# Two attention layers in one kernel: a unit's eight transposes in one place instead of two

## The reference, cut to what matters

```python
# layer 0, per sample
q, k, v = Wq @ y + bq, Wk @ y + bk, Wv @ x + bv          # y = ctx
a = softmax(q_h @ k_h.T / sqrt(E))                       # 8 heads of 32 channels
o = Wo @ (a @ v_h) + bo + x
x1 = (o - mean(o)) * rsqrt(var(o) + eps) * gn_w + gn_b   # over the whole sample
# layer 1, per sample, in chunks of 64 positions
q, k, v = (W_in @ y + b_in).split(3)
p = softmax(q_h.T @ k_h / sqrt(32) + (mask ? 0 : -1e9))  # 64 x 64 per head and chunk
z = (W_out @ (p @ v_h) + b_out) * mask + x1
out = (z - mean(z)) * rsqrt(var(z) + eps)                # over the 2048 positions of a channel
```

## Time and profile before

| | |
|---|---|
| median of 3 runs | 1703.49 us (1701.91 to 1703.87) |
| own time of the profiled execution | 1699.56 us |
| its span from first to last instruction | 1697.7 us |
| mean granted clock of TensorE | 0.988 |
| busy: TensorE, VectorE, ScalarE, GpSimd | 1572.2, 1345.1, 990.8, 471.7 us |

### The profile page before, as it was taken

One profiled execution on the slowest core, in us unless ns is written; L12 is line 12 of the kernel. 1 busy time (PEld: TensorE's weight loads), 2 busy tenths in 40 slices (PEclk: granted clock), 3 DMA queues, 4 the chain that ended last, 5 costly groups with the idle time before them and its releaser, 6 DMA issues.

```text
span 1697.7 us, 56577 instructions
## 1 busy us (share of the span) xinstructions
PE 1572.2 (93%) x23816; PEld 1313.9 (77%) x23816; DVE 1345.1 (79%) x2006; ACT 990.8 (58%) x1779; POOL 471.7 (28%) x293
## 2 busy tenths in 40 slices
PE   3999999999999999999999999999999999999982
PEld 3887787878778787787878778788787878878772
DVE  2777978878787897978878787797978878787884
ACT  3566475565656566475565656566465565656552
POOL 0113224142331313224141331314224142331313
PEclk9999999999999999999999999999999999999996
DMA  5222231323314232231323314232231323314021
GB/s 208 89 74 84 88 105 66 126 82 113 101 45 133 69 125 83 88 105 66 126 82 113 101 45 129 73 122 86 88 109 62 126 82 112 102 46 135 11 76 50
DMA packets 96167, 158.26 MB, mean 93 GB/s; under 512 B 5329, under 2 KB 38225, under 8 KB 95697
## 3 DMA queue, kind: packets, MB, share of 16 engines
q1 hardware_dynamic: 95952, 154.83, 27.8%
HBM read 121.25 MB, written 33.55 MB: 91 GB/s over the span
## 4 chain that ended last, share of the span: by engine, by line
PE 69%; DVE 16%; ACT 8%; issue 5%; DMA 1%; POOL 0%; SPq 0%; ACTq 0%; DVEq 0%; POOLq 0%
PE pj_ps L280 30%; PE l_ps L280 11%; PE l_ps L384 6%; PE s_ps L304 5%; PE w_ps L333 4%; PE w_ps L315 4%; DVE y_lo L675 3%; DVE o_sb L814 2%; ACT y_hi L523 2%; DVE prob L700 2%; PE l_ps L400 2%; ACT o_sb L572 2%; PE s_ps L293 2%; PE l_ps L420 2%; DVE att_lo L717 1%
## 5 line engine op out<-in xcount | busy, mean ns | idle before, releaser
L894 POOL TENSOR_TENSOR prob<-prob,row_inv 128x1024 f32<-128x1024 f32 x128 | 260.1, 2032 | 1001.7 <-DVE row_inv L710 1001.7
L582 ACT CAST att_hi<-w_ps 128x256 fp32r<-128x256 f32 x256 | 82.6, 375 | 292.6 <-PE w_ps L333 288.1
L280 PE MATMUL pj_ps<-y_hi,w_hi 128*128 128x512 f32 x512 | 208.6, 407 | 3.7 <-DVE y_lo L675 3.7
L280 PE MATMUL pj_ps<-y_hi,w_lo 128*128 128x512 f32 x512 | 202.4, 395 | 0.0
L280 PE MATMUL pj_ps<-y_lo,w_hi 128*128 128x512 f32 x512 | 202.4, 395 | 0.0
L693 DVE TENSOR_REDUCE row_max<-s_ps 128x16 f32<-128x1024 f32 x128 | 156.0, 1219 | 56.4 <-PE s_ps L304 54.7
L705 DVE TENSOR_REDUCE row_sum<-prob 128x16 f32<-128x1024 f32 x128 | 154.9, 1210 | 42.6 <-ACT prob L564 42.6
L559 ACT COPY prob_t<-w_ps 128x512 f32<-128x512 f32 x256 | 149.8, 585 | 37.7 <-PE w_ps L315 34.9
L911 POOL TENSOR_TENSOR o_sb<-o_sb,u_sb 128x1024 f32<-128x1024 f32 x64 | 165.6, 2610 | 1.6 <-ACT o_sb L572 1.6
L315 PE MATMUL w_ps<-cst,prob 128*128 128x128 f32 x1024 | 146.9, 274 | 19.2 <-DVE att_lo L717 19.0
L700 DVE TENSOR_TENSOR prob<-s_ps,row_max 128x1024 f32<-128x1024 f32 x128 | 155.3, 1213 | 2.0 <-issue 1.9
(11 more groups left out here) (105 smaller groups left out, 3578.8 us busy)
## 6 DMA issues: line engine op xcount, KB each, us to landing
y_raw<-in_ctx SPq DMA_DIRECT2D x64, 512.0 KB, 4.7
yt_raw<-in_ctx_t SPq DMA_DIRECT2D x64, 512.0 KB, 4.1
x_raw<-in_x SPq DMA_DIRECT2D x64, 512.0 KB, 4.6
out_z<-o_sb SPq DMA_DIRECT2D x64, 512.0 KB, 3.3
mask_b<-in_mask SPq DMA_DIRECT2D x64, 256.0 KB, 3.6
u_sb<-in_w SPq DMA_DIRECT2D x1, 2048.0 KB, 10.5
w_sb<-in_w SPq DMA_DIRECT2D x1, 1024.0 KB, 13.6
cst<-in_consts SPq DMA_DIRECT2D x1, 512.0 KB, 5.4
```

What stands on the lines that cost most here:

```text
L280: last = mm(dst, lhs, rhs, start=i == 0, stop=i == len(todo) - 1)
L894: nc.gpsimd.tensor_tensor(cut, cut, row_inv[:, u % 2, :].unsqueeze(2).to_broadcast([P, 2 * HEADS, CHUNK]), ALU.mult).then_inc(probs_done, 1)
```

## The change

TensorE's four transposes of half 0 leave their place late in the first slot, after the projections and ahead of `layer0` and `wout`, and go to the head of the second slot, directly ahead of the four of half 1. ScalarE's copy of half 0 moves likewise, from its place ahead of the exponents to the head of the second slot. Nothing else is changed.

```diff
@@ TensorE's body @@
                     if e == 1 and not (first and u == 0):
-                        transpose(n, u - 1, 1)
+                        for i in range(2):
+                            transpose(n, u - 1, i)
                     if S_GRAM <= s < S_GRAM + BLOCKS:
                         gram_part(n, s - S_GRAM)
...
                     if s == 0 and not first:
                         variance_over_partitions(n - 1)
-                    if e == 0 and not (first and u == 0):
-                        transpose(n, u - 1, 0)
                     layer0(n, s)
@@ ScalarE's body @@
                     if e == 1 and not (first and u == 0):
-                        copy_pt(n, u - 1, 1)
+                        for i in range(2):
+                            copy_pt(n, u - 1, i)
...
                         copy_v(n, b + 1, j - 2)
-                    if e == 0 and not (first and u == 0):
-                        copy_pt(n, u - 1, 0)
                     if e == 0:
                         exponents(n, u)
```

## The result

The changed kernel takes 1735.06 us (median of 4, 1728.93 to 1739.11) where the kernel before takes 1702.7; the ratio is 1.0192, 95% interval 1.0166 to 1.0218. The forecast was 1687.5, its range ended at 1702. Yet everything that the prediction wanted to see is there.

A forecast was written before the change was run, and what follows sets the result against it. TensorE, busy 93% of the span, was taken as nearly the bound. Gains of 0.47, 0.44 and slot 12's spare 0.16 made 1.07 us in each of 15 samples, 16.0 off 1703.5: 1687.5 us, range 1681 to 1702.

The forecast's parts named there:

- everything that the prediction wanted to see: L400's waits down to about 0.9 us, L315's att_lo waits gone but one, new slot 12 wait about 0.6.
- ScalarE and y_lo, 0.47: In slot 4 the exponents start 0.47 us earlier; through POOL's joins, y_lo in slot 6 and L400 follow by 0.47.
- half: y_lo in slot 6 does not follow POOL, only slot 8 counts: 0.60 us a sample, 9.0, 1694.5; chance 0.14.
- no change: Slot 4's exponents don't move up, copies lengthen ScalarE's slot 5: 0.13 us a sample, 2.0, 1701.5; chance 0.13.
- More: VectorE's o_sb result comes clear of POOL, TensorE sets slot 12: 1.64 us a sample, 24.6, 1678.9; chance 0.09.
- Slot 8, 0.44: Without four transposes ahead of L408, VectorE's run that begins with layer 0's softmax starts 0.44 us earlier.
- Slot 10, 1.17: TensorE's 1.17 us wait at the transposes for att_lo vanishes, with L414 done in the former hole.
- Slot 12, a new wait of 0.57: At the product of x with m (L280), TensorE now arrives early and waits 0.57 us for VectorE's o_bias.
- Net 1.07 a sample, 16.0 in all: Slot 12's product starts 1.07 us earlier in each of 15 samples, 16.0 us together.
- What changes is order on two engines: On TensorE and ScalarE only order changes; no instruction is added or removed, and no DMA moves.
- A run of eight is no new form: Eight transposes in a row on TensorE already stand in slots 0, 4 and 12.
- slower: A slot 12 wait between 1.4 and 2.14 us drops the clock: 1.6 us lost 15 times, 24, 1727.5; chance 0.08.

The follow-up runs named there:

- experiment 3: ScalarE's copies moved as in the changed kernel, TensorE's order as in the kernel before: 1692.61 us, ratio 0.9958 to the kernel before.
- the control with the head at 73: Changed kernel with TensorE's loop head pinned at place 73 of its block, where it lay anyway: 1729.13 us, ratio 1.0177.

## Why the prediction was wrong, step by step

**ScalarE and y_lo, 0.47: right.** In the sample from 550 of the changed kernel the exponents of slot 4 stand right behind the Q copy (timeline of ScalarE), VectorE's y_lo is shorter and ends 1.08 behind POOL's joins, as before (timelines of VectorE and GpSimd):

```profile
583.08 0.69 ACT L543 ACTIVATE q_s<-pj_ps,col 128x512 f32<-128x512 f32 x1 [0.71 <-PE pj_ps L280]
583.66 1.05 ACT L563 ACTIVATE prob<-prob 128x1024 f32<-128x1024 f32 x1
```

```profile
591.86 2.16 DVE L673 TENSOR_TENSOR y_lo<-y_raw,y_hi 128x1024 fp32r<-128x1024 f32 x1
```

```profile
588.20 4.74 POOL L909 TENSOR_TENSOR o_sb<-o_sb,u_sb 128x1024 f32<-128x1024 f32 x2
```

588.20 + 4.74 = 592.94, and the chain has y_lo end at 594.02. Against the earlier trace rows y_lo lost 0.49 us, the whole saving and not half of it, and experiment 3 gave 0.47 a sample. L400's waits fell by more, 0.65 on the mean. By the records T1 starts 7.20 us behind the scores of slot 6 instead of 7.68, which is the 0.47 again; the rest is TensorE itself, which in the changed order comes to T1 0.18 later. The rivals "half" and "no change" fall with it: both banks' copies in one slot cost nothing that shows. "More" falls in slot 12: the wait is there, and so is VectorE's long o_sb result:

```profile
620.08 2.58 DVE L812 TENSOR_SCALAR o_sb<-o_sb,z_rstd,z_shift 128x512 f32<-128x512 f32 x2
```

**Slot 8, 0.44: right.** VectorE's idle time before the run of layer 0 fell from 0.86 to 0.43:

```profile
605.95 0.61 DVE L747 SCALAR_TENSOR_TENSOR a<-v_row,col,l_ps 128x128 f32<-128x128 f32 x2 [0.43 <-PE l_ps L408]
```

**Slot 10, 1.17: right.** The timeline of TensorE has the output product directly behind the U product, where the earlier trace rows had the wait:

```profile
613.32 0.81 PE L414 MATMUL l_ps<-w_sb,a 128*128 128x256 f32 x3
614.07 0.49 PE L280 MATMUL pj_ps<-att_hi,w_hi 128*128 128x512 f32 x1
```

**Slot 12, a new wait of 0.57: right in kind, and near in size.** 9.3 us in 14 waits are 0.66 each. The chain there:

```profile
624.36 0.16 DVE o_bias L763
624.53 0.25 issue
624.77 3.01 PE l_ps L280 x12
```

**Net 1.07 a sample, 16.0 in all: near, where the loop's head is in time.** 14.9 with the last unit left out, 13.7 and 12.5 between the kernels with the head at 0 and at 100: 1 to 3.5 us under the sum. With 0.66 in place of 0.57 in slot 12 the sum is 14.7.

**"What changes is order on two engines", costed at nothing: the step that failed.** I gave the order a price only through data: who waits for whose result. Its price through the code was not in the sum. With the loop's head where it lay, a run of eight at the end of the loop in place of four, product, four made the head late in each of the 13 jumps back: +21.5 at L293, +11.2 at L333, and +20.5 of slower matmuls in the profiled execution. "A run of eight is no new form" was true of the slots named, none of which stands ahead of the branch. The time, 1735.06, lies beyond every rival.

**The rival "slower"** named the clock, but from a wait in slot 12, which stayed at 0.7. The clock did fall, behind stands of 1.47, 1.98, 2.04, 1.72 and 1.56 us at the loop's head; it didn't behind others of 1.38 to 1.98. In the control with the head at 73 it fell behind one of 1.13 us (and the hole at the value products that follows it), so the 1.4 us that I took as harmless from the earlier trace rows is no bound.

**What stays open.** Why the order moves the edge from under 55 to over 60. TensorE's stream waits 2.15 us for x_lo, 64 instructions ahead of the branch. With the last block 60 ahead its start is passed just behind that wait, with 65 just ahead of it. But this moment alone does not decide: from the wait on both kernels have the same instructions, and in all 13 jumps of both it ends 3.44 to 3.46 us ahead of the branch. The records show one difference behind it. The wait ahead of slot 15's V product (L356), 39 instructions ahead of the branch, is passed 3.33 us ahead of the branch in every jump of the kernel before, and 3.15 in every jump of the changed one; in the one late pass at 64 it is 3.18, in the other twelve 3.33. So these late passes lose 0.15 to 0.18 us in the stretch in which the last block begins. Whether that is part of the cause or another effect of it, no run tells. Why the clock falls behind some stands and not behind others as long wasn't settled either.

## What to carry to other kernels

Where a loop's body is as long as this one (some 3060 instructions on TensorE, 12 or 13 code packets a pass), look at the first instruction of the loop in the trace before and after any reordering: a row "issue", as often as the loop jumps back, was code that came late here. Undo the change in the last unit alone to tell this from the change's own effect. The place of the loop's head is worth a scan by itself: here 100 in place of 73 took 0.7% off the kernel as it was, and the changed kernel at 100 is 1.4% under the kernel as it was.

## What the runs showed of the hardware

- With the hint, the loop's head was fetched in time only where the last block of 256 instructions began far enough ahead of the branch: 14 was too late in all 13 passes, 87 in none, and between them the order of the same instructions decided (60: late in 13 or in none). Late means the head's packet begins 0.9 to 2.2 us behind the branch and TensorE stands 1.1 to 2.3 us.
- With the hint removed the price is about the same (2.7%) as that of the order that makes the hint come to nothing (1.8 to 2.3%).
- Stands of nearly the same sum cost little clock in one kernel (21.1 us at the head, busy time +3.9 us, the order of before at 27) and much in another (21.5 us, +20.5, the changed kernel).
